# Two 16-wide cross attentions: scores in two half-array pieces with the peak products between them, and 6 of 64 peak banks read by ScalarE and GpSimd

## The reference, cut to what matters

```
q = _split_heads(query_modal @ Wq.T + bq)        # 2 x 16 heads x 256 tokens x 16
k = _split_heads(key_value_modal @ Wk.T + bk)    # 2 x 16 heads x 4096 tokens x 16
v = _split_heads(key_value_modal @ Wv.T + bv)
scores = jnp.einsum('bhnd,bhmd->bhnm', q, k) * HEAD_DIM ** -0.5
attn = jax.nn.softmax(scores, axis=-1)
x = jnp.einsum('bhnm,bhmd->bhnd', attn, v)
return x.transpose(0, 2, 1, 3).reshape(query_modal.shape) @ Wo.T + bo
```

## Time and profile before

| | us |
|---|---|
| median of 3 runs (lowest, highest) | 3470.1 (3467.83, 3473.94) |
| the profiled execution, its own time | 3471.26 |
| its span, first to last instruction | 3469.5 |
| mean granted TensorE clock, whole span | 0.971 |
| busy: TensorE matmul, VectorE, ScalarE, GpSimd | 3199.3, 2147.4, 1804.9, 847.7 |
| VectorE's reductions of L2x_psm and L3x_psm (L1271) | 287.5 and 287.5 |
| the exponentials of L2x and L3x (L1248) | 248.2 and 248.1 |

### The profile page before, as it was taken

The page is one execution under the profiler, slowest core; times in us unless marked ns, Lnnn a source line. Parts: engine busy times, 40 slices in busy tenths (PEclk is TensorE's granted clock), DMA queues, the critical chain, the costliest instruction groups (busy, mean ns, idle before and its releaser), DMA issues. The chain is left out here.

```text
span 3469.5 us, 55920 instructions
## 1 busy us (share of the span) xinstructions
PE 3199.3 (92%) x21581; PEld 2074.6 (60%) x21616; DVE 2147.4 (62%) x3342; ACT 1804.9 (52%) x2609; POOL 847.7 (24%) x654
## 2 busy tenths in 40 slices
PE   8989999999999999999769799999988889999689
PEld 6855696666666666666436686444455644445565
DVE  4336314666666666665487405999754289995764
ACT  4436212666666666667356231676735137676741
POOL 1042001444444444445157103000030120000440
PEclk9999999999999999999889899999999989999899
DMA  6259462000010000000686436766200495650110
GB/s 210 103 198 304 184 266 88 10 1 10 10 37 22 1 10 10 1 1 1 165 301 242 149 126 181 162 124 124 51 27 25 134 244 117 124 118 25 49 78 12
DMA packets 231636, 351.01 MB, mean 101 GB/s; under 512 B 104384, under 2 KB 177792, under 8 KB 226256
## 3 DMA queue, kind: packets, MB, share of 16 engines
q1 hardware_dynamic: 230992, 346.38, 34.2%
q0 software_dynamic: 384, 1.05, 0.1%
HBM read 261.35 MB, written 86.05 MB: 100 GB/s over the span
## 5 line engine op out<-in xcount | busy, mean ns | idle before, releaser
L1816 DVE TENSOR_REDUCE L1x_pk<-L1x_psm 128x2 f32<-128x1024 f32 x236 | 289.1, 1225 | 302.4 <-PE L1x_psm L1578 302.4
L1517 POOL TENSOR_TENSOR L1x_acc<-L1x_acc,L1x_pr 128x512 f32<-128x512 f32 x256 | 354.3, 1384 | 376.1 <-ACT L1x_pr L1749 358.0
L1749 ACT ACTIVATE L1x_pr<-L1x_pss 128x1024 f32<-128x1024 f32 x272 | 263.9, 1022 | 154.0 <-PE L1x_pss L1595 153.9
L1248 ACT ACTIVATE L3x_pr<-L3x_pss 128x1024 f32<-128x1024 f32 x256 | 248.1, 1021 | 107.2 <-PE L3x_pss L1143 106.9
L1248 ACT ACTIVATE L2x_pr<-L2x_pss 128x1024 f32<-128x1024 f32 x256 | 248.2, 1021 | 103.1 <-PE L2x_pss L1143 102.8
L1271 DVE TENSOR_REDUCE L3x_pk<-L3x_psm 128x1 f32<-128x512 f32 x448 | 287.5, 685 | 15.3 <-PE L3x_psm L1100 11.7
L1846 DVE TENSOR_TENSOR L1x_acc<-L1x_acc,L1x_pr 128x512 f32<-128x512 f32 x256 | 276.3, 1079 | 32.0 <-ACT L1x_pr L1749 19.5
L1271 DVE TENSOR_REDUCE L2x_pk<-L2x_psm 128x1 f32<-128x512 f32 x448 | 287.5, 685 | 11.3 <-PE L2x_psm L1100 7.7
L1739 ACT COPY L1x_pss<-L1x_neg 128x1024 f32<-128x1024 f32 x272 | 272.9, 1028 | 1.3 <-DVE L1x_pk L1816 1.3
L1608 PE MATMUL L1x_pso<-L1x_pr,L1x_V 128*64 128x256 f32 x2176 | 253.1, 383 | 0.6 <-DVE L1x_OT L1855 0.6
L1554 PE MATMUL L1x_psm<-L1x_cT,L1x_w 128*128 128x512 f32 x512 | 247.7, 606 | 4.7 <-DVE L1x_dm L1833 2.8
(11 more groups left out here) (765 smaller groups left out, 5838.6 us busy)
## 6 DMA issues: line engine op xcount, KB each, us to landing
f0e_wt<-in_f_pieces SPq DMA_DIRECT2D x10, 3072.0 KB, 11.4
offset_rows<-s_rows SPq DMA_DIRECT2D x32, 768.0 KB, 5.9
L2x_KS<-L2x_key_parts SPq DMA_DIRECT2D x24, 1024.0 KB, 12.9
L3x_KS<-L3x_key_parts SPq DMA_DIRECT2D x24, 1024.0 KB, 13.0
s_add<-offset_rows SPq DMA_DIRECT2D x32, 512.0 KB, 7.3
n_cT<-in_ctxT SPq DMA_DIRECT2D x32, 512.0 KB, 4.7
f1e_wt<-in_f_pieces SPq DMA_DIRECT2D x8, 2048.0 KB, 13.2
L2x_key_parts<-n_kst SPq DMA_DIRECT2D x32, 384.0 KB, 3.1
```

The costliest lines, as they stand in the source:

```text
L1248: nc.scalar.activation(pr[:, a % RING, :, :].rearrange("p h q -> p (h q)"), pss[:, 2 * (a % 2):2 * (a % 2) + 2, :].rearrange("p x q -> p ( ...
L1517: i = nc.gpsimd.tensor_tensor(acc[:, n, 1, :, :], acc[:, n, 1, :, :], pr[:, a % RING, :, 1, :], ALU.add)
L1749: nc.scalar.activation(pr[:, a % RING, :, :, :].rearrange("p h e q -> p (h e q)"), pss[:, x:x + 2, :].rearrange("p h n -> p (h n)"), ACT.E ...
L1816: nc.vector.reduce_max(pk[:, m, qt, :, j], peak_banks(z, qt), AX).then_inc(peak_read, 1)
```

## The change

It has five parts.

1. **Two pieces for a score.** The 97 rows are split. Piece 0 holds four of the six pairs (64 rows), piece 1 the other two and the ones (33 rows). Both pieces of heads 0 and 1 lie on partitions 0 to 63, those of heads 2 and 3 on 64 to 127. So a slot has 8 score matmuls in place of 4, each on one half of the array's rows.
2. **One product at a time.** A slot's first product (array rows 0 to 63) stands before the slot's score pieces of the other half, and its second (rows 64 to 127) beside the last two pieces of the first half. Each claims its bank alone.
3. **Six of 64 banks leave VectorE.** ScalarE copies them to SBUF (`off`), and GpSimd folds them into one maximum with three instructions a step (subtract, clip at 0, add), `higher`. VectorE reads the folded 256 columns once a unit (`OFF_COLUMN`), after a wait for `folds`.
4. **The rows go through a transfer.** The four peak rows come from one bank with two matmuls at slot 27. VectorE copies them once (4x256) to `lows`, and SyncE sends them to partitions 32 and 96 of `QS` (`row(n)`). The scores of a unit wait for `row_here`.
5. **Twice as many, half as large transfers** for `QS` (12 for 6) and `KS` (6 for 3 a unit); the two fills of ones become four.

The new transfer of the rows of unit 0 stands behind the one of V of unit 0 on the one queue. The diff, cut to its core:

```diff
@@ SyncE
+            def row(n):
+                b = n // NU
+                sp.wait_ge(turn_read, counts[row_turn[n]])
+                sp.dma_start(QS[ONE:64 + ONE + 1:64, 1, n % NU * 2:n % NU * 2 + 2, b * S:(b + 1) * S], lows[:, n % 2, :]).then_inc(row_here, 16)
...
             values(0)
+            row(0)
             stack(1)
@@ GpSimd
+            def higher(out, one, other, room):
+
+                fold(nc.gpsimd.tensor_tensor(room, one, other, ALU.subtract))
+                fold(nc.gpsimd.tensor_scalar(room, room, 0.0, None, ALU.max))
+                fold(nc.gpsimd.tensor_tensor(out, other, room, ALU.add))
+
+            for n in range(1, UNITS):
+                for j in range(1, OFF_J):
+                    c = OFF_J * (n - 1) + j
+                    pool.wait_ge(turn_copied, c + 1)
...
+                higher(top[:, n % 2, 0:256], top[:, n % 2, 0:256], top[:, n % 2, 256:512], above[:, 0:256])
@@ TensorE
-                    pe.wait_ge(turn_read, x - 2)
+                    pe.wait_ge(turn_copied if by_act[x - 3] else turn_read, counts[x - 3])
...
+            def score(n, s, g, h, z):
+
+                a, b = n * STEPS + s, n // NU
+                at = slice(64 * h, 64 * h + (64, ONE + 1)[z])
+                return nc.tensor.matmul(pss[:, 2 * (a % 2) + h, g * S:(g + 1) * S], KS[at, n % 2, z, g, s * P:(s + 1) * P],
+                                        QS[at, z, n % NU * 2 + g, b * S:(b + 1) * S], start=(z == 0), stop=(z == 1), skip_group_check=True)
+
+            def scores_beside_products(n, s):
...
+                if last:
+                    product(m, first)
                 if s == 0:
-                    pe.wait_ge(turn_read, rows_out[n])
-                    pe.wait_ge(ks_in[n % 2], 16 * 3 * (n // 2 + 1))
+                    pe.wait_ge(row_here, 16 * (n + 1))
+                    pe.wait_ge(ks_in[n % 2], 16 * 6 * (n // 2 + 1))
...
+                score(n, s, 0, 1, 0)
+                score(n, s, 0, 1, 1)
+                for z in range(2):
+                    score(n, s, 0, 0, z)
+                    score(n, s, 1, 1, z)
+                if last:
+                    product(m, first + 1)
+                score(n, s, 1, 0, 0)
+                score(n, s, 1, 0, 1).then_inc(scored, 1)
@@ ScalarE
+                nc.scalar.copy(off[:, c % 4, :], psm[:, x % 3, :]).then_inc(turn_copied, 1)
@@ VectorE
                     if i == NP - 1:
-                        dve.wait_ge(turn_read, x + 1)
+                        dve.wait_ge(folds, n * FOLDS)
+                        link(nc.vector.reduce_max(pk[:, n % 2, OFF_COLUMN, 0:NJ], top[:, n % 2, 0:256].rearrange("p (j e) -> p j e", j=NJ), AX))
+                        dve.wait_ge(turn_read, counts[x])
                         nc.vector.reduce_max(mx[:, n % 2, :], pk[:, n % 2, :, :], AX).then_inc(peak, 1)
...
-                    nc.vector.tensor_copy(QS[ONE:ONE + 1, h0 + 2 * e:h0 + 2 * e + 2, b * S:(b + 1) * S],
-                                          psm[ONE:ONE + 1, x % 3, :].rearrange("p (h q) -> p h q", h=2)).then_inc(turn_read, 1)
+                nc.vector.tensor_copy(lows[:, n % 2, :], psm[0:UH, x % 3, 0:S]).then_inc(turn_read, 1)
```

More of the change, by code:

```diff
@@ L31 @@
 NH = 16
-ROOM = 40
+ROOM = 44
 NUMBERS = {}
@@ L978, in peak_of, with column, off_number, order_of_turns @@
             return i // (2 * 2 * QT), i // 4 % QT, i // 2 % 2 + 2 * (i % 2)
+        def column(h, qt):
+            return 4 * (h % 2) + 2 * (h // 2) + qt
+        def off_number(n, i):
+            return OFF_J * (n - 1) + i // 8 if n >= 1 and i % 8 == OFF_AT and i < 8 * OFF_J else None
+        def order_of_turns():
+            def product(n, i):
+                c = off_number(n, i)
+                return ("dve", None) if c is None else ("act", c)
+            for i in range(LATE):
+                yield product(1, i)
+            yield "row", 0
+            for i in range(LATE, AHEAD):
+                yield product(1, i)
+            for n in range(UNITS):
+                for x in range(SLOTS):
+                    if n == UNITS - 1 and x % 4 == 2 and x // 4 < UNITS - 1:
+                        yield "dve", None
+                    m, first, last = of_slot(n, x)
+                    for i in range(first, last):
+                        yield product(m, i)
+                    if x == ROW_SLOT and n + 1 < UNITS:
+                        yield "row", n + 1
+            yield "dve", None
         def wide_banks(x):
@@ L988, in of_slot @@
             return (m, i, i + NP // SLOTS) if m < UNITS else (m, 0, 0)
+        turns = list(order_of_turns())
+        by_act = [kind == "act" for kind, _ in turns]
+        counts = [1 + sum(o == by_act[x] for o in by_act[:x]) for x in range(len(turns))]
+        offs = [x for x, o in enumerate(by_act) if o]
+        row_turn = {n: x for x, (kind, n) in enumerate(turns) if kind == "row"}
         @block.sync
@@ L1028, in _ @@
             for s, part in enumerate(QPART):
[L1029 removed]
+                for a in range(2):
+                    at = 64 * a + s // 2 % 2 * 2 * hd + s % 2
+                    sp.dma_start(QS[at:at + 2 * hd - 1:2, s // 4, :, :].rearrange("p (x g) s -> p x (g s)", g=2),
+                                 qscratch[part].rearrange("c (x r a g) s -> a r (c x) (g s)", r=hd, g=2, a=2)[a]).then_inc(qs_in, 16)
             for j in range(NCH):
@@ L1045, in _ @@
                 leading(n + 2)
+                row(n + 1)
                 sp.wait_ge(scored, STEPS * (n + 1))
@@ L1049, in _ @@
                 values(n + 2)
+            row(UNITS - 1)
         @block.gpsimd
@@ L1086, in first_products, with may_read_keys, product @@
                 i.then_inc(wide, 1)
[L1088 to L1101 removed]
+            def may_read_keys(n):
+                pe.wait_ge(kh_in[n % 2], 32 * (n // 2 + 1))
+                if n == 1:
+                    pe.wait_ge(wide_read, NP // 2)
+                if n < NU:
+                    pe.wait_ge(masked, n + 2)
+                    pe.wait_ge(masked_more, n)
+            def product(n, i):
+                b, y = divmod(n, NU)
+                r = i % 2
+                j, qt, h = peak_of(i - r)
+                if i == 0:
+                    may_read_keys(n)
+                x = claim()
+                nc.tensor.matmul(psm[:, x % 3, :], QM[64 * r:64 * r + 64, y, h, b * S + qt * P:b * S + (qt + 1) * P],
+                                 KH[64 * r:64 * r + 64, n % 2, j * 512:(j + 1) * 512], start=True, stop=True).then_inc(turn, 1)
             def picked(i):
@@ L1115, in rows @@
                 pe.wait_ge(peak, n + 1)
-                for e in range(2):
-                    x = claim()
-                    for h in range(2):
-                        for qt in range(QT):
-                            hq = (2 * e + h) * QT + qt
-                            i = nc.tensor.matmul(psm[ONE:ONE + 1, x % 3, h * S + qt * P:h * S + (qt + 1) * P], mx[:, n % 2, hq:hq + 1],
-                                                 k.less[:, :], start=True, stop=True)
-                    i.then_inc(turn, 1)
-                rows_out[n] = taken[0]
+                x = claim()
+                for qt in range(QT):
+                    i = nc.tensor.matmul(psm[0:UH, x % 3, qt * P:(qt + 1) * P], mx[:, n % 2, qt::QT], k.less[:, :], start=True, stop=True)
+                i.then_inc(turn, 1)
             def denominators(n):
@@ L1263, in written @@
                 taken[0] += 1
-                dve.wait_ge(turn, x + 1)
+                if not by_act[x]:
+                    dve.wait_ge(turn, x + 1)
                 return x
```

145 lines of the change are left out of this document (79 added, 66 removed).

## The result

| | before | after |
|---|---|---|
| median, us (lowest, highest) | 3468.97 (3465.03, 3473.94) | 3443.50 (3439.65, 3447.93) |
| ratio, 95% interval | | 0.9933 [0.9915, 0.9952] |
| the profiled execution, span | 3471.26, 3469.5 | 3447.93, 3446.1 |
| VectorE, ScalarE, GpSimd busy | 2147.4, 1804.9, 847.7 | 2067.6, 1848.8, 1161.9 |
| a unit, first exponential to first exponential | 43.37 | 41.24 |

The account below looks back on a forecast made before the run. VectorE and TensorE were both taken to be at their limit. A layer: -18.5 + 5.9 + 2 + 0.5 = -10.1 us, two layers -20.2, giving 3450 us; forecast's own range 3438 to 3462, overall 3427 to 3484.

Parts of the forecast that it names:

- A pair of slots, 2.38: TensorE's work for two slots falls from 2.61 to 2.38 us, as two of four change-overs are saved.
- A unit, 40.5: Unit falls from 43.37 to 40.5 us, 0.3 of it for missed claims; folded reduction, peaks, row copy fall where VectorE is late.
- VectorE, 0.654 a bank: VectorE's reductions take 0.654 us each, at its limit before; after the change its unit sums to 39.5 us.
- ScalarE and GpSimd, cost 0: ScalarE's six copies and GpSimd's folds cost nothing; at worst 0.6 and 0 to 1 us a unit.
- Rows inside a unit, cost 0: Peak rows' transfer, 3.1 us, lands before the next unit's scores; if late, up to 1 us a unit.
- Start of unit 0, +5.9 a layer: Unit 0's row waits behind V's transfer, so four slots of scores come after V: +5.9 us, bounds +1 and +9.
- rival (b): Unit 0's row overtakes V, so the start costs +1 in place of +5.9: 3440 us; chance 0.1.
- Unit 7, +2: Halves idle in slots without products, 1.6 us, and denominators need a change-over, 7 x 0.1: +2 a layer, bounds +1 and +4.
- Lead-in, +0.5: Six more QS transfers hold back the next context load, mostly hidden: +0.5 us a layer, bounds 0 and +3.6.
- Rival (a): TensorE's halves don't overlap when lengths differ: slot 0.86 us, unit 45.2, total 3512, slower; chance 0.15.
- (c): Gaps in TensorE's stream come oftener, one in every second unit: +20 us, 3470, no change; chance 0.15 including (d).
- (d): The change does little: bank claims still bind as pairs, units at 42 us, 3468; counted in (c)'s 0.15.

Follow-up runs that it names:

- four_mends: Changed kernel with later copy, unit 0's rows ahead of V, V alone on the queue, pieces alternating in slots without products: 3427.78 us, 0.9892 of before.
- offload_after_exp: Kernel before with only the six banks a unit moved off VectorE, ScalarE's copy behind its slot's exponential: 3473.21 us, 1.0016 of before.
- offload_only: Kernel before with only the six banks a unit moved to ScalarE and GpSimd, ScalarE's copy ahead of the exponential: 3533.34 us, 1.0199 of before.

## Why the prediction was right, and where not

- **A pair of slots, 2.38: measured 2.42 and 2.49.** The mechanism held: half-height pieces run beside products, two change-overs of four are gone. A slot on TensorE is 0.67, not 0.645, and the way of one bank (product, reduction, release: 1.17 us) then binds the pairs that VectorE reads alone. The forecast had only the engines' sums.
- **A unit, 40.5: measured 41.24.** The forecast had 0.3 for claims that miss; the one stall at the copy was 1.07 by itself, by the run with the later copy. A unit without it is 40.17. The step that failed is "falls where VectorE is late": the copy's place in VectorE's order was not set against the averages' new place in TensorE's.
- **VectorE, 0.654 a bank and "at its limit": wrong.** It reads four banks in 2.48 us, (2.48 - 0.68) / 3 = 0.60 each. The 0.654 of the earlier trace rows was TensorE's pace of four banks in 2.61 us seen on VectorE, whose short waits don't show as idle time. That both bound the kernel before was wrong too: relief on VectorE alone gave +0.16% there and left pairs without a copy at 2.61; after the change it gave -0.19 us a unit. The gain is there without the offload, 43.37 to 41.43: 13 pairs shorter by 0.12 (1.6 us), the two at the peaks by 1.25 together (3.98 + 2.63 to 2.65 + 2.71), and the one at the start longer by 0.94. The peaks are a term that the forecast had only as work of VectorE, not as a wait of TensorE: before, the rows stood in two of the three banks, and the next pair of products waited for the second cast. Timeline of before:

```profile
2221.59 0.39 PE L1100 MATMUL L2x_psm<-L2x_KH,L2x_QM 64*128 64x512 bf16 x2 [0.66 <-DVE L2x_QS L1290]
```

  After, the rows hold one bank for one copy of 0.40. That part of the change was not tried apart, so its share of the 1.25 is argued, not shown.
- **ScalarE and GpSimd, cost 0:** held. GpSimd's instructions took 1.28 and 1.48 us over 512 columns (estimate 1.38 and 1.4), and the folded reduction (0.41) waited for nothing visible; its own time makes the peaks' pair 2.98 where it is 2.65 without it. But ScalarE's copy is free only because the product stands ahead of the scores.
- **Rows inside a unit, cost 0:** held; issued at 2303.41, some 4 us ahead of the next unit's scores.
- **Start of unit 0, +5.9 a layer: measured +3.5 and +2.7** to the first averages (80.36 and 79.09 us after the stage's first transfer, 76.86 and 76.39 before), or +4.5 and +2.2 from V's issue (12.6 in both layers; 8.1 and 10.4 before). Of the working, this term is the most too large. The row did wait for V, landing with it at 2183.2 and not at 2185.5: V was issued 1.9 us earlier on this scale and took 7.2 us, not 7.7. And in L3x V had taken 10.3 us before and took 7.4 now, which the forecast had left as it was. Slots at half clock took 1.3, as forecast. Scores came at 2183.20, so rival (b) fell.
- **Unit 7, +2: measured +1.6** (36.74 and 35.12 us from first to last exponential), for another reason. Pairs with denominators take 2.84 in place of 2.64, the others 1.99 in place of 1.97. Idle halves are ruled out by four_mends; what is left is the second change-over around the denominators, 0.2 and not 0.1, which was not tried apart.
- **Lead-in, +0.5:** no cost seen; V of L2x was issued 67.8 us after the stage's first transfer, 68.8 before.
- **The sum.** From a stage's first transfer to the output projection L2x lost 13.4 us and L3x 16.3, 29.7 where 20.2 were forecast. The ordinary units saved less each (2.13 in place of 2.9), but the earlier trace rows has unit 4 at 46.68 and L3x its like at 46.09, and both gaps are gone: units 1 to 5 saved 13.8 and 13.9 us, where 14.5 were forecast, and some 3 of that are the gap. (Unit 6 saved 1.4 of 1.5.) The gaps are no chance of one profile: `offload_after_exp` has them again in unit 4 of both layers (47.38 and 48.05), `offload_only` has none in unit 4, and the ten profiles with half-height pieces have none anywhere. What makes them stays open. Unit 0 saved more, since it too had been disturbed (50.09 us in L3x). Against that stands a term that the forecast lacked: the rest of the program took 6.3 us more in this profile. Nearly all of it is behind L3x. From its last exponential to the end of the span the ten profiles with half-height pieces have 293.8 to 298.0 us, the three without them 289.3 to 290.7. Two loads land later there in all ten. `m_A` takes 5.6 to 6.3 us from issue to landing and not 4.3 to 4.4, and TensorE waits for it (timelines of TensorE, 3196 to 3203 us of before and 3167 to 3174 us of after):

```profile
3198.12 5.42 PE L3971 MATMUL m_ps<-NT,m_win 128*128 128x512 f32 x12 [0.61 <-DMA m_A<-in_m_A_log]
```

```profile
3170.41 4.13 PE L4085 MATMUL m_ps<-NT,m_win 128*128 128x512 f32 x9 [2.01 <-DMA m_A<-in_m_A_log]
```

  The first weights of `f3e_wt` take 4.9 to 6.1 us and not 4.1 to 4.4, and TensorE's wait for them is 2.4 to 3.5 us and not 1.5 to 1.8. Together that is about 3 of the 5.8 us. The granted clock is lower too at much the same point of the work (windows of before and after, 40 to 60 us behind the last exponential), but the first of these waits comes ahead of it, 21 us behind the last exponential, where the granted clock is 1.00 in both:

```profile
3218.80:3238.80 20.00, 7.00 (x22) 3.21 (x21) 13.31 (x10) 9.09 (x7) 0.00 (x0) 0.74 0.51 211
```

```profile
3189.70:3209.70 20.00, 8.70 (x20) 3.15 (x18) 11.56 (x9) 7.79 (x7) 0.00 (x0) 0.66 0.53 211
```

  What makes the loads land later, and what the clock costs by itself, stays open. The total came out 6.5 us off the forecast with terms off by 0.7 a unit, 3 a start, and 6 in the rest, against gaps that went away unforecast: that the sum lies so near is in part luck.
- **Rival (a)** fell: pieces of 256 columns start inside a product. **(c)** fell, and the other way round: the change adds matmuls, and the gaps went away. **(d)** fell with the units.

## What to carry to other kernels

With few buffers between two engines, find the way of one buffer (write, read, release), and what is written behind the instruction that waits for it: every order of a pair of slots tried here costs 1.17 us plus that where VectorE reads the first bank, and 1.06 plus that, or TensorE's own 2.42, where ScalarE does. When work moves in one engine's order, set each instruction that waits for it on another engine against its new place; one line was worth as much as half of the change. A pace read from a busy engine is not its own until it has been seen where nothing feeds it late.
